# A token-and-image network on one core: joined-stage outputs left by pixels, running sums in place of block statistics, and a first Fourier layer that turns no rows

## The reference

```python
x = x + ttt(gn(x))          # layer norm, q/k/v projections, scan over chunks of 16 tokens, norm, W_o
x = x + fourier(gn(x), L1)  # rfft2, two block-diagonal complex layers (4 groups of 128), times spectrum, irfft2
x = x + gate(gn(x), L2)     # box means -> small convs -> two fully connected layers -> sigmoid per channel
x = x + fourier(gn(x), L3)

def _ttt_linear(...):
    XQ, XK, XV = rope(heads(xn @ q_w.T)), rope(heads(xn @ k_w.T)), heads(xn @ v_w.T)
    def step(carry, inp):                 # 256 steps per image, 8 heads of 64
        Z1 = xk @ W1c + b1c
        grad = _ln_l2_bwd(Z1, xv - xk, g, bb)
        Attn1 = tril(xq @ xk.T)
        Z1_bar = xq @ W1c - et * Attn1 @ grad + b1_bar
        W1n = W1c - (last_eta * xk).T @ grad
        return ((W1n, b1n), xq + _ln(Z1_bar, g, bb, EPS_IN))
    ...
    return _ln(out, post_w, post_b, EPS_IN) @ o_w.T
```

## Time and profile before

| | |
|---|---|
| median of 3 runs | 5464.71 us (5461.24 to 5465.51) |
| profiled execution, its own time | 5460.91 us |
| its span | 5458.9 us |
| PE busy | 5180.7 us, 95% |
| DVE busy | 4166.4 us, 76% |
| ACT busy | 2608.8 us, 48% |
| POOL busy | 2701.1 us, 49% |
| joined stage, scan steps with leaving tiles | about 1674 to 3691 us of the span |
| first Fourier layer | about 3784 to 4622 us |
| last Fourier layer | from about 4655 us |

### The profile page before, as it was taken

How to read it: one execution, slowest core, us unless ns; L and a number is a source line. 1 busy time by engine, 2 the same in 40 slices (tenths; PEclk the granted TensorE clock), 3 DMA queues, 4 the chain that set the end, 5 groups by cost and what they waited for, 6 DMA issues and landing times. The chain is left out here.

```text
span 5458.9 us, 134572 instructions
## 1 busy us (share of the span) xinstructions
PE 5180.7 (95%) x44534; PEld 3979.9 (73%) x44534; DVE 4166.4 (76%) x14714; ACT 2608.8 (48%) x7573; POOL 2701.1 (49%) x4382
## 2 busy tenths in 40 slices
PE   6999999999979999999999999997999996899998
PEld 3444444444448888888888888886899986799998
DVE  6766667655668888888888888885888888566665
ACT  0111111111147777777777777773555554454444
POOL 1444444444446666666666666662444543333332
PEclk8999999999979999999999999998999998899999
DMA  5434444433334444444444444443122211222221
GB/s 209 165 123 161 147 145 158 135 125 122 112 103 124 128 127 127 128 129 127 127 127 128 127 128 128 127 127 133 75 84 95 79 80 50 90 95 81 90 82 78
DMA packets 599450, 644.80 MB, mean 118 GB/s; under 512 B 172981, under 2 KB 503101, under 8 KB 587869
## 3 DMA queue, kind: packets, MB, share of 16 engines
q1 hardware_dynamic: 440844, 491.84, 27.8%
q10 hardware_dynamic: 157904, 144.22, 7.9%
HBM read 357.96 MB, written 278.00 MB: 117 GB/s over the span
## 5 line engine op out<-in xcount | busy, mean ns | idle before, releaser
L1628 PE MATMUL proj_ps<-proj_w_sb,proj_h 128*128 128x512 f32 x3072 | 1346.4, 596 | 0.0
L1628 PEld LDWEIGHTS proj_ps<-proj_w_sb,proj_h 128*128 128x128 f32 x3072 | 577.0, 190 | 742.1 <-issue 723.2
L1506 DVE SCALAR_TENSOR_TENSOR proj_lin<-proj_ps,proj_rstd,proj_wbias_sb 128x512 f32<-128x512 f32 x384 | 283.2, 746 | 492.9 <-PE proj_ps L1628 487.0
L1913 POOL TENSOR_TENSOR scan_b_step<-scan_core,scan_rate_last 128x128 f32<-128x128 f32 x512 | 331.7, 648 | 593.9 <-DVE scan_core L2145 593.9
L2354 PE MATMUL scan_ps_y<-scan_o_t,proj_wo_sb 128*128 128x128 f32 x4096 | 566.2, 281 | 2.1 <-ACT scan_o_t L2009 2.1
L2354 PEld LDWEIGHTS scan_ps_y<-scan_o_t,proj_wo_sb 128*128 128x128 f32 x4096 | 496.7, 191 | 32.3 <-ACT scan_o_t L2009 2.6
L1421 POOL TENSOR_TENSOR proj_gk<-proj_rec,proj_gain_sb 128x256 f32<-128x256 f32 x256 | 181.2, 728 | 526.4 <-DVE proj_rec L1527 526.4
L1982 ACT ACTIVATE scan_square<-scan_ps_z 128x64 f32<-128x64 f32 x1024 | 219.0, 219 | 460.0 <-PE scan_ps_z L2273 456.4
L1415 POOL TENSOR_TENSOR proj_by_cos<-proj_lin,proj_rope 128x512 f32<-128x512 f32 x256 | 335.9, 1326 | 162.8 <-DVE proj_lin L1506 121.1
L2285 PE MATMUL scan_ps_w<-scan_step,scan_record 64*128 64x128 f32 x4088 | 354.0, 292 | 14.8 <-DVE scan_step L2150 14.0
L1975 ACT COPY scan_state_w<-scan_ps_w 128x512 f32<-128x512 f32 x480 | 278.8, 581 | 122.3 <-PE scan_ps_w L2285 121.3
(11 more groups left out here) (326 smaller groups left out, 13190.2 us busy)
## 6 DMA issues: line engine op xcount, KB each, us to landing
scan_record<-records SPq DMA_DIRECT2D x259, 392.0 KB
records<-proj_rec ACTq DMA_DIRECT2D x256, 392.0 KB, 3.7
spectra<-fourier_spec SPq DMA_DIRECT2D x16, 2112.0 KB, 6.4
fourier_spec<-spectra SPq DMA_DIRECT2D x16, 2112.0 KB, 8.5
proj_h<-x SPq DMA_DIRECT2D x32, 1024.0 KB, 6.7
queries<-proj_q ACTq DMA_DIRECT2D x128, 256.0 KB, 3.9
gradients<-scan_stored SPq DMA_DIRECT2D x512, 64.0 KB
scan_q_in<-queries SPq DMA_DIRECT2D x128, 256.0 KB, 7.8
```

Of the source, the lines that this page charges most:

```text
L1506: v.scalar_tensor_tensor(lin[q][:, n], ps[q][n][:], rstd[k][:, j:j + 1], T.wbias[:, n], ALU.mult, ALU.add).then_inc(lin_sb.sem, 1)
L1628: last = pe.matmul(ps[j % 2][n][:], h[k][:, ct, j * P:(j + 1) * P], T.w[:, n, ct], start=ct == 0, stop=ct == CT - 1)
L1913: v.tensor_tensor(b_step[g][:], core[g][:], rate_last[g][:, :, 2:3].broadcast_to([P, PB, HD]), ALU.mult).then_inc(b_step_sb[g].sem, 1)
```

## The change

The tile products of the joined stage are taken the other way round: the turned rows `o_t` are now the stationary operand and 512 columns of `T.wo` stream past, so the result has pixels on partitions. One ScalarE copy of 512 columns takes it out. The norm weights post_w and post_b are applied when ScalarE copies the turned rows (four activations of 128 columns with scale and bias instead of one copy), so `opening` folds nothing into `wo`. In place of bn_stats VectorE adds the tile and its squares to running totals (`totals`), ScalarE makes the squares (`output_tile_squares`), and 32 one-column products at the end give the means. `x1` is now (image, token, channel), so the first Fourier layer loads its unit with pixels on partitions, as 4096 pieces of 512 bytes, and multiplies directly with F1: `turn_rows` and its copies are gone. In that layer ScalarE now copies the transformed columns into `spec`, and VectorE does 13 boxes in the column phase; the squares of the finished spectrum move on ScalarE from the column phase into the chunks.

```diff
@@ fourier_forth, ScalarE
-                for n in range(NB2):
-                    evacuate(u, n, packed[n][1] * P)
-                    if n in (3, 5, 7):
-                        energy_of_last(u, 1 - k, n // 2 - 1)
-                evacuate(u, SYM, 2 * P)
+                evacuate(u, 0, packed[0][1] * P)
+                for n, (s, m) in enumerate(slots):
+                    evacuate(u, n + 1, packed[n + 1][1] * P if n + 1 < NB2 else 2 * P)
+                    act.wait_ge(dft_ps.sem, dft_ps.at(u, PRE + n + 1))
+                    nc.scalar.copy(spec[k][:, s:s + m].rearrange("p s r h -> p (s r h)"), psD[n % 2][:, 0:m * P]).then_inc(col_sb.sem, 1)
...
                 for c in range(NCH):
                     if not last and c < NB1:
                         row(u, k, c)
-                        if c + 2 < NB1:
-                            evacuate(u, ROW + c + 2)
+                    if c < 4:
+                        energy_of_last(u, 1 - k, c)
@@ fourier_forth, VectorE
-                for n, (s, m) in enumerate(slots):
-                    dve.wait_ge(dft_ps.sem, dft_ps.at(u, PRE + n + 1))
-                    v.tensor_copy(spec[k][:, s:s + m].rearrange("p s r h -> p (s r h)"),
-                                  psD[n % 2][:, 0:m * P]).then_inc(col_sb.sem, 1)
...
+                dve.wait_ge(prod_sb.sem, prod_sb.at(u, 0))
+                boxed = 13
+                for g in range(boxed):
+                    box_of_last(u, 1 - k, g)
@@ fourier_forth, TensorE
-            def turn_rows(u, i, k):
-                transposes(u, ROW + i, [xb[k][:, (4 * i + j) * P:(4 * i + j + 1) * P] for j in range(4)])
+            def rows(u, t, k, i):
+                for j in range(4):
+                    done = pe.matmul(psD[t % 2][:, j * P:(j + 1) * P], xb[k][:, 4 * i + j], F1, start=True, stop=True)
+                done.then_inc(dft_ps.sem, 1)
@@ opening, VectorE
-            dve.wait_ge(wo_folded, 1)
-            steps.then(dve, v.tensor_copy(T.wo_bias[:], ps_small[:, 2]))
-            for ct in range(CT):
-                steps.then(dve, v.tensor_scalar(T.wo[:, ct], T.wo[:, ct], vecs[:, 2, ct:ct + 1], None, ALU.mult))
+            steps.then(dve, v.tensor_copy(T.post[:], vecs[:, 2:4]))
+            dve.wait_ge(wo_in, 16)
@@ scan_and_read, ScalarE
-                a.copy(o_t[:], ps_turn[:]).then_inc(o_t_sb.sem, 1)
+                for ct in range(CT):
+                    done = a.activation(o_t[:, ct], ps_turn[:, ct], ACT.Identity, scale=T.post[:, 0, ct:ct + 1], bias=T.post[:, 1, ct:ct + 1])
+                done.then_inc(o_t_sb.sem, 1)
...
-                for n in range(CT):
-                    done = a.activation(y_sb[par][:, b * CT + n], ps_y[:, n], ACT.Identity, bias=T.wo_bias[:, n:n + 1])
-                done.then_inc(y_done.sem, 1)
+                a.copy(y_sb[par][:, b], ps_y[:]).then_inc(y_done.sem, 1)
+
+            def output_tile_squares(tile):
...
+                a.activation(y_sq[t % 2][:], y_sb[par][:, b], ACT.Square).then_inc(y_sq_sb.sem, 1)
@@ scan_and_read, VectorE
-                for n in range(CT):
-                    where = stats6[:, b * CT + n, bass.ds(sc, 1), :].rearrange("p o e -> p (o e)")
-                    v.bn_stats(where, y_sb[par][:, b * CT + n]).then_inc(stats_sb.sem, 1)
+                v.tensor_tensor(total[:, b, 0], total[:, b, 0], y_sb[par][:, b], ALU.add).then_inc(total_sb.sem, 1)
+                dve.wait_ge(y_sq_sb.sem, y_sq_sb.at(t, 1))
+                v.tensor_tensor(total[:, b, 1], total[:, b, 1], y_sq[t % 2][:], ALU.add).then_inc(total_sb.sem, 1)
@@ scan_and_read, TensorE
-                for ct in range(CT):
-                    pe.matmul(ps_y[:, n], T.wo[:, ct, n * P:(n + 1) * P], o_t[:, ct], start=ct == 0, stop=False)
+                pe.matmul(ps_y[:], o_t[:, n], T.wo[:, n], start=n == 0, stop=n == CT - 1, skip_group_check=True)
```

More of the change, by code:

```diff
@@ L155, in sig @@
             return Signal(ctx, nc, f"{name}_{n}", per, credit)
-        xb = [sb(f"x{k}", [P, TOK]) for k in range(2)]
+        xb = [sb(f"x{k}", [P, TOK // P, P]) for k in range(2)]
         wt = sb("weights", [P, CT, 4, P])
@@ L378, in _ @@
             act.wait_ge(cleared.sem, cleared.at(0, 1))
-            for n in range(NB1):
-                evacuate(0, n - PRE)
             loop(unit)
-            evacuate(UNITS - 1, ROW, 2 * P)
+            act.wait_ge(turned_ps.sem, turned_ps.at(UNITS, 1))
+            act.wait_ge(dft_ps.sem, dft_ps.at(UNITS - 1, PRE + ROW - 1))
+            nc.scalar.copy(turned[0][:, 0:2 * P], psT[0][:, 0:2 * P]).then_inc(turned_sb.sem, 1)
+            act.wait_ge(dft_ps.sem, dft_ps.at(UNITS - 1, PRE + ROW + 1))
+            symmetric(1, ROW)
             act.wait_ge(col_sb.sem, col_sb.at(UNITS, 1))
@@ L553, in transform_rows @@
                     pe.wait_ge(row_sb.sem, row_sb.at(u, NB1 + i - 1))
-                transforms(u, ROW + i, [(j * P, j, F1) for j in range(4)])
+                rows(u, ROW + i, k, i)
             def turn_columns(u, n):
@@ L611, in unit @@
                     mix1(u, k, ct, c)
-                    if not last:
-                        turn_rows(u, c, 1 - k)
                 for c in range(NCH):
@@ L1197, in _ @@
                       start=True, stop=True).then_inc(averaged, 1)
-            pe.wait_ge(wo_in, 16)
-            pe.wait_ge(var_made, 1)
-            for ot in range(CT):
-                for ct in range(CT):
-                    last = pe.matmul(ps_small[:, 2, ot:ot + 1], T.wo[:, ct, ot * P:(ot + 1) * P], vecs[:, 3, ct:ct + 1],
-                                     start=ct == 0, stop=ct == CT - 1)
-            last.then_inc(wo_folded, 1)
 def project(nc, T, K, x_in, rope, group_mean, gn_now, rec, q_out, images=B, groups=TOK // 512):
@@ L1700, in scan_and_read @@
         x_sb = [sb(f"x_in{q}", [P, UNITS, P]) for q in range(2)]
-        y_sb = [sb(f"y{q}", [P, UNITS, P]) for q in range(2)]
+        y_sb = [sb(f"y{q}", [P, B, C]) for q in range(2)]
+        y_sq = [sb(f"y_sq{q}", [P, C]) for q in range(2)]
+        total = sb("total", [P, B, 2, C])
+        mean_of = sb("mean_of", [P, 1])
+        chan_mean_sq = sb("chan_mean_sq", [P, UNITS])
         q_t = sb("q_t", [P, HP, P])
@@ L2095, in body @@
                         outputs_turned(proj)
+                    if gone:
+                        output_tile_squares(gone)
                 if scan:
@@ L2220, in body @@
                     if gone:
-                        moments(gone)
+                        totals(gone)
                 elif norm:
@@ L2236, in _ @@
             loop(dve, body)
-            dve.wait_ge(stats_sb.sem, stats_sb.at(TILES, 0))
-            for u in range(UNITS):
-                v.bn_aggr(chan_stats[:, u, :], stats6[:, u].rearrange("p s e -> p (s e)"))
+            dve.wait_ge(means_ps.sem, means_ps.at(0, 1))
+            now = ps_y[:, 0:2 * UNITS].rearrange("p (u e) -> p u e", e=2)
+            steps.then(dve, v.tensor_copy(chan_stats[:], now))
+            steps.then(dve, v.tensor_tensor(chan_mean_sq[:], chan_stats[:, :, 0], chan_stats[:, :, 0], ALU.mult))
+            steps.then(dve, v.tensor_tensor(chan_stats[:, :, 1], chan_stats[:, :, 1], chan_mean_sq[:], ALU.subtract))
         @block.tensor
@@ L2405, in _ @@
             loop(pe, body)
+            pe.wait_ge(total_sb.sem, total_sb.at(TILES, 0))
+            pe.wait_ge(y_done.sem, y_done.at(TILES, 0))
+            pe.wait_ge(mean_made.sem, mean_made.at(0, 1))
+            for b in range(B):
+                for ct in range(CT):
+                    for e in range(2):
+                        n = (b * CT + ct) * 2 + e
+                        done = pe.matmul(ps_y[:, n:n + 1], total[:, b, e, ct * P:(ct + 1) * P], mean_of[:], start=True, stop=True)
+            done.then_inc(means_ps.sem, 1)
 def norm_factors(nc, name, gmean, grstd, gstd, gn, coef):
```

108 lines of the change are left out of this document (51 added, 57 removed).

## The result

The changed kernel takes 5529.0 us (median of 4 runs, 5526.9 to 5534.0), the kernel before 5464.6 us in the same rounds (5461.2 to 5465.5): ratio 1.0121, 95% interval 1.0109 to 1.0133, so 1.2% slower. A second measurement on another occasion gave 5523.0 us and 1.0112 (1.0094 to 1.0131). The prediction was 5517 us.

The account below looks back on a forecast made before the run. TensorE was taken to bound the joined stage and first Fourier layer, VectorE nearly as much in the joined stage. 83 - 18 - 1 - 5.6 - 2 = +56 on 5460.9 gave 5517 us, range 5430 to 5620.

Parts of the forecast that it names:

- Joined stage, +83: VectorE's two additions, partly blocked by GpSimd, lengthen each period by 0.69 us over 120 tiles: +83 us.
- addition first: Joined stage: the first addition runs before GpSimd's `stored`; list +1.05 us, period +0.69 us; chance 0.40.
- slack of 0.36: Joined stage: VectorE's list of 16.46 us in a period of 16.82 us has 0.36 us to spare.
- Period 17.5: Sign in the joined stage: the period of `zg` is 17.5 us, or 18.1 if `stored` goes first.
- Fourier layer, -18: First Fourier layer, 15 units: 3.4 us of turns saved, 1.5 and 0.8 lost, about 1.2 a unit: -18 us.
- first hidden sum 1.5 us late: First Fourier layer: 13 boxes with `xsum` take 12.7 us, delaying VectorE's first hidden sum by 1.5 us.
- End of the joined stage, -5.6: 16 bn_aggr (14.22 us) go; 64 products and small work come to 8.6 us: -5.6; +1.6 at half clock.
- Opening, -2: Opening: scaling of `wo`, 2.05 us at the end of VectorE's list, goes: -2 us.
- first rows, -1: First rows of the Fourier layer: turns gone, -3.4; first load in 512-byte pieces, +2.3; together -1 us.
- `stored` first: Rival, joined stage: GpSimd's `stored` goes before the first addition, +156 us there, total 5590 us; chance 0.28.
- Ports free: Rival: joined-stage additions find the SBUF ports free and the boxes fit their phase; total 5410 us; chance 0.16.
- The whole 3.4 us kept: Rival: the Fourier layer keeps 3.4 us a unit while the joined stage loses 83; total 5483 us; chance 0.10.

Follow-up runs that it names:

- Experiment 1: Changed kernel with the two VectorE additions of the joined stage replaced by reductions to sums per group, one SBUF input each: 5455.8 us, ratio to the kernel before 0.9983.
- experiment 3: Kernel before with only `wo` unscaled, norm weights applied to turned rows in four ScalarE activations, one copy for outputs: 5459.0 us, ratio 0.9993.
- experiment 4: New Fourier-layer split alone in the kernel before: 5466.6 us, ratio 1.0006; changed kernel with the old split, rows unturned: 5549.1 us, ratio 1.0154.

## Why the prediction came out as it did

The sign, the mechanism and the largest term were right; that the total of 5517 came as near to 5529 as it did is partly luck, because errors of both signs cancelled.

- **Joined stage, +83: measured +87.9.** The order was the one I had taken as likelier, addition first: 126 of the 128 first additions run undisturbed. The ground for it was thin, since the row at 2499.04 is one of 16 among the 128 `L2166` of the kernel before that weren't stretched; most take 0.89. The by-hand list matches the trace: `zgain` ending 2.70 us behind the start of the first addition was forecast, 2.61 is shown (6.62 + 1.71 less 5.72). Over 2000 to 2400 us the mean of an addition is 0.69 and 0.96 us, of `t_row` 0.33 in place of 0.29, eight a period. So the list grew by 0.44 for the additions' length, 0.27 for the second one's wait and 0.31 for `t_row`: 1.02, where 1.05 was forecast. Of the slack of 0.36 only 0.2 was used up: VectorE still waits 3.6 us for ScalarE in 2000 to 2400 us, 0.16 a period. The pieces then come to about 0.8 where 0.73 was measured; the stretch holds two of the four periods with a second addition of 1.76 us, which makes it a little more than the mean of the stage. Experiment 1 shows that the blocking is what costs: without it 65 of the 88 us are gone. The 23 that stay are the longer list and the sums over eight tiles; ScalarE's four activations have no part in them (experiment 3).
- **The signs told beforehand.** Period 17.5: 17.57. TensorE at about 93%: 94%. VectorE's wait for ScalarE "gone": the 4.6 us of the earlier trace rows are 1.6 in the same stretch. Additions or `t_row` over 0.3 us more: yes. A unit about 1.2 us shorter: 2.1.
- **Fourier layer, -18: measured -31.3. Mis-sized.** The step "first hidden sum 1.5 us late" was 0.6. Thirteen boxes with `xsum` took 11.7 us in place of 12.7, since only eight boxes met an `xsum`, and the hidden sum needs no wait behind them. TensorE's waits grew by 1.0 us a unit, where 2.3 had been subtracted (3.4 - 1.5 - 0.8 is 1.1, which the sum rounded up to 1.2); a unit got 2.1 shorter, so 0.3 of the 3.4 is in neither. The waits also show a term that I had put at nothing: TensorE waits 0.9 us a unit for the turned columns that ScalarE copies, where it had waited 0.4 for VectorE's copies; the waits for hidden sums grew from 0.5 to 1.1. What I also had wrong is the part of the split: I booked it as what costs 1.3 of the 3.4, and experiment 4 shows that it costs nothing by itself and saves 1.2.
- **End of the joined stage, -5.6: measured +2.6.** The products took 10.9 us (64 of them), at a granted clock of 0.63, between the 7.2 us that the sum had and the 14.3 us that I had named for half the clock (+1.6). The rest is in the drain: the last `zg` to the first of these products is 76.2 us, where 70.9 led to the first bn_aggr. A tile's last steps follow each other there. The four activations for turned rows (1.5 us for `o_t`) make 2.1 of these 5.3 us by experiment 3; for the square, the additions and GpSimd's part in them (1.76 us for the second addition of five tiles) 3.2 are left, not separated. I had given the end 0.5 us *less* for ScalarE's copies.
- **Opening, -2, and first rows, -1:** -1.9 and -1.3.
- **Projection stage, no term: +16.9.** The prediction had nothing here. A stage without an edit was taken to stay as it is, and this is the largest error of the sum. It was hidden by the Fourier layer's extra 13 us. The loaded and scaled rows reached TensorE later, and the stage has TensorE's waits 9.2 us longer and a clock shortfall of 8.5 us to show for it; why the loads land later stays open.
- **Rest, no term: -6.3.** Of this 3.0 is the last unit, by the new split (experiment 4). Another 4.1 lies in the last Fourier layer, from its first hidden sum to the end (789.5 to 785.4 us); the other kernels have 785.0 to 788.8 there, and the cause is open. Between the two it is 0.8 longer.
- **Rivals.** `stored` first (5590) did not occur as the rule. "Ports free" (5410) is refuted by the blocked rows. The whole 3.4 us kept (5483): no, 2.1 were.

## What to carry to other kernels

When work moves between forms on VectorE, count the inputs that it reads from SBUF, not only its columns: a form with one SBUF input (bn_stats, a reduction, an operand in PSUM) can lie beside GpSimd, one with two can't, and it then also stops covering for what comes behind it. Look at what the removed instruction was standing in front of before moving the new one elsewhere. And compare stages that have no edit too: a total that comes out right may hold terms that cancel.

## What the runs showed that I had not expected

- A stage with no edit became 12 to 18 us longer in nine profiles of nine, with its 2 MB loads landing after 8.9 to 9.0 us in place of 8.0 to 8.4; the DRAM address of `x1` has no part in it.
- A wait of TensorE of 2.3 us can be followed by a lower granted clock at once: 0.84 as a mean over the 10 us from 190 to 200, in which TensorE was still busy for 7.7 us. It isn't always so. Of the nine waits, those of 2.27, 3.71, 2.35, 2.20 and 2.17 us had it behind them, those of 2.52, 2.08, 2.90 and 2.62 us did not, so the length of the wait alone doesn't decide. The kernel before, with waits of up to 1.7 us, stayed at 1.00. Over the nine stretches the clock's shortfall adds up to 8.5 us, the waits to 9.2 us more than before: 17.7, near the 16.9 that the stage got longer. The same account fits the second profile of the changed kernel: 8.1 and 5.1 us for 12.5 longer.
- Moving the additions out of GpSimd's way made `t_row`, two instructions of 64 columns, take 1.67 us in the row shown. On the mean of 2000 to 2400 us one `t_row` takes 0.383 us, against 0.278 in experiment 1 and 0.326 in the changed kernel: 0.84 lost a period of eight, where the changed kernel loses 0.38 there and 0.28 at its second addition. The difference, 0.18, is what the period grew by.
